# Pair stage of a four-layer graph network: part of the one-hot and row work moved from VectorE to ScalarE and GpSimd

## The reference

```python
def _sage(x, src, dst, Wn, bn, Wr):
    msg = x[src]
    agg = segment_sum(msg, dst, N)
    deg = segment_sum(ones, dst, N)
    mean = agg / maximum(deg, 1.0)[:, None]
    return mean @ Wn + bn + x @ Wr

h = relu(_sage(x, src, dst, W1n, b1n, W1r) + (x @ Wl1 + bl1))
out = _sage(h, src, dst, W2n, b2n, W2r) + (h @ Wl2 + bl2)
x = layernorm(x + out)
```

## Time and profile before

| | us |
|---|---|
| median of 3 runs | 3620.97 (3620.26 to 3625.03) |
| the profiled execution | 3621.94 |
| its span | 3620.1 |

### The profile page before, as it was taken

How to read it: one execution, slowest core, us unless ns; L and a number is a source line. 1 busy time by engine, 2 the same in 40 slices (tenths; PEclk the granted TensorE clock), 3 DMA queues, 4 the chain that set the end, 5 groups by cost and what they waited for, 6 DMA issues and landing times.

```text
span 3620.1 us, 122165 instructions
## 1 busy us (share of the span) xinstructions
PE 2921.0 (81%) x50473; PEld 2635.8 (73%) x50473; DVE 2935.5 (81%) x4757; ACT 2188.2 (60%) x5856; POOL 1429.5 (39%) x1204
## 2 busy tenths in 40 slices
PE   0199999999999789899787787887767888887886
PEld 0177777777777689899677777777756777777775
DVE  7599999999999733233588878988857999999997
ACT  6334444444444410000598888898867989899887
POOL 2000000000000000000298988998973666666564
PEclk9999999999999999999899999999977988889897
DMA  8157777777777799888687777887738888888884
GB/s 220 66 154 234 232 231 226 226 228 229 236 231 226 250 346 366 334 325 325 220 279 255 264 257 250 262 268 244 264 125 286 291 277 278 280 281 275 272 278 135
DMA packets 606666, 907.43 MB, mean 251 GB/s; under 512 B 358505, under 2 KB 494858, under 8 KB 587163
## 3 DMA queue, kind: packets, MB, share of 16 engines
q1 hardware_dynamic: 583992, 800.62, 67.7%
q10 hardware_dynamic: 19763, 94.38, 7.2%
q0 software_dynamic: 2352, 4.52, 0.3%
HBM read 651.96 MB, written 247.40 MB: 248 GB/s over the span
## 4 chain that ended last, share of the span: by engine, by line
DVE 37%; PE 28%; issue 12%; ACT 10%; DMA 7%; POOL 6%; ACTq 0%; DVEq 0%; SPq 0%; POOLq 0%
PE ps L1054 8%; PE ps L671 5%; DVE EDG L861 4%; DMA U<-AD 4%; DVE U L842 4%; DVE U L1824 3%; POOL EDG L1275 3%; ACT U L1634 3%; DVE EDG L1762 2%; PE ps L684 2%; PE ps L697 2%; ACT U L1336 2%; POOL EDG L1267 2%; DVE U L834 2%; PE ps L1296 2%
## 5 line engine op out<-in xcount | busy, mean ns | idle before, releaser
L561 ACT ACTIVATE U<-ps 128x512 bf16<-128x512 f32 (+1 forms) x637 | 356.3, 573 | 559.8 <-PE ps L684 535.6
L1634 ACT ACTIVATE U<-U,T 128x65 f32<-128x65 f32 x1806 | 460.1, 342 | 48.6 <-PE ps L1695 43.6
L1054 PE MATMUL ps<-U 128*128 128x192 bf16 x4802 | 418.0, 248 | 32.8 <-DMA U<-AD 32.4
L1267 POOL TENSOR_TENSOR EDG<-U,edge 128x512 f32<-128x512 f32 (+1 forms) x196 | 212.6, 1090 | 584.7 <-DVE edge L1419 550.8
L1054 PEld LDWEIGHTS ps<-U 128*128 128x128 bf16 x4802 | 402.8, 98 | 41.6 <-DMA U<-AD 38.4
L671 PE MATMUL ps<-U 128*128 128x98 bf16 (+1 forms) x5292 | 365.4, 224 | 34.1 <-DVE U L842 34.1
L671 PEld LDWEIGHTS ps<-U 128*128 128x128 bf16 x5292 | 339.4, 98 | 57.5 <-DVE U L842 55.6
L1662 POOL TENSOR_TENSOR U<-U 128x455 f32<-128x455 f32 x258 | 296.9, 1154 | 213.0 <-DVE U L1824 213.0
L861 DVE TENSOR_TENSOR EDG<-edge,EDG 128x1792 bf16<-128x1792 bf16 x343 | 366.2, 1079 | 13.7 <-DMA OSD<-EDG 12.4
L1303 PE MATMUL ps<-U 128*128 128x65 bf16 x7203 | 288.2, 195 | 73.8 <-DVE A L1396 72.8
L697 PE MATMUL ps<-EDG,U 128*128 128x193 bf16 x2401 | 311.5, 249 | 35.8 <-ACT U L561 24.6
(11 more groups left out here) (322 smaller groups left out, 6923.6 us busy)
## 6 DMA issues: line engine op xcount, KB each, us to landing
U<-ROWS SPq DMA_DIRECT2D x411, 448.0 KB, 4.7
U<-AD SPq DMA_DIRECT2D x98, 1568.0 KB, 8.5
OND<-EDG SPq DMA_DIRECT2D x343, 224.0 KB, 2.8
OSD<-EDG SPq DMA_DIRECT2D x343, 224.0 KB, 3.5
AD<-U ACTq DMA_DIRECT2D x49, 1568.0 KB, 5.5
EDG<-ROWS SPq DMA_DIRECT2D x171, 448.0 KB, 6.1
U<-OND SPq DMA_DIRECT2D x303, 224.0 KB, 5.7
U<-OSD SPq DMA_DIRECT2D x213, 224.0 KB, 4.8
```

What stands on the lines that cost most here:

```text
L561: ev4.by(act.activation(prow[i % NPW][:, P * g:P * (g + m)], ps[4 + gg % 2][:, 0:P * m], ACT.Copy))
L1054: ins = pe.matmul(ps[q][:, 0:192], arow[r][:, P * j:P * j + P], (XsB if p else XsA)[:, j, :, :].rearrange("p s f -> p (s f)"), start=(j == ...
L1634: ins = act.activation(V4[k % NV][:, 0, c, :], H[k % NHR][:, c, :], ACT.Copy, scale=a4[d % 2][:, s:s + 1])
```

## The change

Five pieces of work change their engine. The slot conversion of L850 goes to ScalarE, just ahead of L584 and L585. The mean of L878 goes to ScalarE, just behind the copy of X. Of the 14 one-hot columns of each `hots`, the last two of the target part, c = 5 and 6, are made by ScalarE as Relu(1 - |slot - r|): two Abs of 128 elements with the slot as pointer bias, a wait for its own engine, and one Relu over both. VectorE makes the other 12. Stores and counts wait for both. ScalarE copies the second half of the layer's output from PSUM to one of two new buffers (`xadd`), and GpSimd adds it to X, ahead of the bias. On VectorE the semaphore `summed` now comes with the reciprocal.

```diff
 pairs_sp:
+                sp.wait_ge(hot_b.at, hot_b.o + k + 1)
 pairs_pool, biased(i):
+                pool.wait_ge(t_out.at, i + 1)
+                x_in.by(pool.tensor_tensor(X[:, i, :], X[:, i, :], xadd[i % 2], ALU.add))
                 pool.wait_ge(x_in.at, i + 1)
 pairs_act, dense(i, n):
                     cat_x.by(act.activation(cat[q][:, D:P], X[:, i, :], ACT.Copy))
+                    act.wait_ge(summed.at, i + 1)
+                    cat_d.by(act.activation(cat[q][:, 0:D], A[:, i, 0:D], ACT.Copy, scale=rdeg[:, i:i + 1]))
...
-                    t_out.by(act.activation(T[:, i, 0:D], ps[7][:, 2 * P:2 * P + D], ACT.Copy))
+                    act.activation(T[:, i, 0:D], ps[7][:, 2 * P:2 * P + D], ACT.Copy)
+                    if i >= 2:
+                        act.wait_ge(x_in.at, i - 1)
+                    t_out.by(act.activation(xadd[q], ps[7][:, 2 * P + D:3 * P], ACT.Copy))
 pairs_act:
+            def hots(i, b):
+                k = NH7 * i + b
+                r = k % NHB
+                if k >= NHB:
+                    kk = k - NHB
+                    act.wait_ge(count4.at, NG4 * (kk // NH7) + (7 * (kk % NH7) + 6) // 4 + 1)
+                    act.wait_ge(hot_st[r].at, 32 * (k // NHB))
+                act.wait_ge(slot_ea.at, i + 1)
+                for c in (5, 6):
+                    ac.by(act.activation(OD[r][:, c, :], iota1, ACT.Abs, scale=-1.0, bias=E3[:, i, 1, 7 * b + c:7 * b + c + 1]))
+                act.wait_ge(ac.at, ac.n)
+                hot_b.by(act.activation(OD[r][:, 5:7, :], OD[r][:, 5:7, :], ACT.Relu, bias=1.0, scale=-1.0))
...
-                    act.wait_ge(slot_ev.at, e + 1)
+                    act.wait_ge(slot_mm.at, 2 * e + 2)
+                    if e >= 2:
+                        act.wait_ge(hot8.at, NH7 * (e - 1))
+                    slot_ev.by(act.activation(sdb[e % 2].rearrange("p b s c -> p s b c"),
+                                              bc(ps[3][:, 0:2 * NB].unsqueeze(2), [P, 2 * NB, 2]), ACT.Identity, bias=sc[:, 41:42]))
...
                     count(i, 2)
+                    hots(i, 2)
                 if d is not None:
                     dense(d, 3)
                     dense(d, 12)
                 if i is not None:
+                    hots(i, 3)
                     count(i, 3)
 pairs_pe, count(i, n):
                 pe.wait_ge(hot8.at, NH7 * i + (g + m - 1) // 7 + 1)
+                pe.wait_ge(hot_b.at, hot_b.o + NH7 * i + (g + m + 1) // 7)
 pairs_pe, dense, n == 2:
-                        pe.wait_ge(x_in.at, i)
+                        pe.wait_ge(t_out.at, i)
 pairs_dve:
-            def slots(e):
...
-                hot8.by(dve.tensor_tensor(HOT[r].rearrange("p s c (r k) -> p (s c) r k", k=2), bc(r1v.unsqueeze(1), [P, 14, D, 2]),
+                hot8.by(dve.tensor_tensor(HOT[r].rearrange("p s c (r k) -> p (s c) r k", k=2)[:, 0:12, :, :], bc(r1v.unsqueeze(1), [P, 12, D, 2]),
...
-                    summed.by(dve.tensor_scalar(nod[:, 1, i:i + 1], ps[6][:, 3 * D:XW], 1.0, None, ALU.max))
-                    dve.wait_ge(summed.at, i + 1)
-                    dv.by(dve.reciprocal(rdeg[:, i:i + 1], nod[:, 1, i:i + 1]))
-                elif n == 3:
...
-                    cat_d.by(dve.tensor_scalar(cat[q][:, 0:D], A[:, i, 0:D], rdeg[:, i:i + 1], None, ALU.mult))
-                elif n == 11:
-                    dve.wait_ge(t_out.at, i + 1)
-                    x_in.by(dve.tensor_tensor(X[:, i, :], X[:, i, :], ps[7][:, 2 * P + D:3 * P], ALU.add))
+                    summed.by(dve.reciprocal(rdeg[:, i:i + 1], nod[:, 1, i:i + 1]))
```

More of the change, by code:

```diff
@@ L469, in gnn_kernel @@
         x_ok = on(spl_a, 2)
+        hot_b = on(ld_x, 32)
+        xadd = [part(o2 + 6272 + D * i, D) for i in range(2)]
         over_in, over_t, bounds_t = sem("over_in"), sem("over_t"), sem("bounds_t")
@@ L575, in pairs_act @@
                     off_ev.by(act.activation(offb, ps[2][0:CP, 256:256 + NB], ACT.Identity, bias=sc[0:CP, 40:41]))
+                if i is not None:
+                    hots(i, 0)
                 if d is not None:
@@ L578, in pairs_act @@
                     count(d, 11)
+                if i is not None:
+                    hots(i, 1)
+                if d is not None:
                     count(d, 12)
@@ L601, in pairs_act @@
                     count(i, 4)
+                    hots(i, 4)
                 if d is not None:
@@ L605, in pairs_act @@
                     count(i, 5)
+                    hots(i, 5)
                 if d is not None:
@@ L609, in pairs_act @@
                     count(i, 6)
+                    hots(i, 6)
                     count(i, 7)
@@ L844, in fields @@
                 (fld_hot if c1 == HC else dv).by(ins)
-            def slots(e):
-                dve.wait_ge(slot_mm.at, 2 * e + 2)
-                if e >= 2:
-                    dve.wait_ge(hot8.at, NH7 * (e - 1))
-                slot_ev.by(dve.tensor_scalar(sdb[e % 2].rearrange("p b s c -> p s b c"),
-                                             bc(ps[3][:, 0:2 * NB].unsqueeze(2), [P, 2 * NB, 2]), -1.0, None, ALU.add))
             def hots(i, b):
@@ L860, in hots @@
                     dve.wait_ge(hot_st[r].at, 32 * (k // NHB))
-                hot8.by(dve.tensor_tensor(HOT[r].rearrange("p s c (r k) -> p (s c) r k", k=2), bc(r1v.unsqueeze(1), [P, 14, D, 2]),
-                                          bc(sdb[i % 2][:, b, :, :].rearrange("p s (c k) -> p (s c) k", k=2).unsqueeze(2), [P, 14, D, 2]),
+                hot8.by(dve.tensor_tensor(HOT[r].rearrange("p s c (r k) -> p (s c) r k", k=2)[:, 0:12, :, :], bc(r1v.unsqueeze(1), [P, 12, D, 2]),
+                                          bc(sdb[i % 2][:, b, :, :].rearrange("p s (c k) -> p (s c) k", k=2)[:, 0:12, :].unsqueeze(2), [P, 12, D, 2]),
                                           ALU.is_equal))
@@ L870, in dense @@
                     dv.by(dve.tensor_copy(deg[:, i:i + 1], ps[6][:, 3 * D:XW]))
[L871 to L876 removed]
+                    dv.by(dve.tensor_scalar(nod[:, 1, i:i + 1], ps[6][:, 3 * D:XW], 1.0, None, ALU.max))
                     own()
[L878 to L881 removed]
+                    summed.by(dve.reciprocal(rdeg[:, i:i + 1], nod[:, 1, i:i + 1]))
             for t in range(LAST):
@@ L899, in pairs_dve @@
                             fields(jb, (3, 8).index(n), 5, HC)
-                    if e is not None and n == 1:
-                        slots(e)
-                    if d is not None and n < 11:
+                    if d is not None:
                         dense(d, n)
@@ L905, in pairs_dve @@
                         hots(i, (n + 1) // 2)
-                    if d is not None and n == 11:
-                        dense(d, n)
             dve.wait_ge(x_ok.at, x_ok.o + NB)
```

2 lines of the change are left out of this document (removed).

## The result

The changed kernel took 3644.33 us (median of 4 runs, 3643.74 to 3651.91), the kernel before 3622.41 beside it (4 runs, 3620.26 to 3625.03). The ratio is 1.0064, interval 1.0048 to 1.008: slower by 22 us. The forecast was 3657 (+36), range 3585 to 3682.

A forecast was written before the change was run, and what follows sets the result against it. VectorE was taken as full, TensorE close behind and waiting on ScalarE's evictions. 20.46 + 0.88 + 0.32 + 0.93 = 22.59 us a step against 21.80, +0.79 over 45 steps, gave 3657 us; range 3585 to 3682, the forecast's own 3638 to 3680.

The forecast's parts named there:

- Limits: Pair-stage step of 21.80 us: VectorE's own limit falls to 20.3 us, TensorE's without waits for VectorE is 20.46.
- TensorE's removable wait: TensorE's loads waiting for VectorE's field products (L842) and source one-hots (L820): 1.34 us a step would go.
- Term 1: Run offsets: first hot pair between offset copy and count group 10 eviction delays TensorE's use by 0.88 us a step.
- Term 2: Slot numbers: ScalarE's slot conversion lengthens the gapless chain to the load TensorE waits for by 0.32 us a step.
- Term 3: Row transfers: ROWS issues hold ScalarE, delaying the fourth pair and count group 3 eviction; +0.93 us a step.
- c: Start of ScalarE's count 1 eviction, the zero point for the times in the row-transfer chain.
- it lasts 1.20: Length in us taken for the second ROWS issue, read from the kernel before the change; it would end at c + 3.22.
- The other four pairs: Remaining hot pairs on ScalarE, behind the count 3 eviction: priced zero, or 0.2 us a step if cover is thinner.
- No change: Rival A: ROWS issues do not hold up the fourth pair; 3619 us, within 3605 to 3630; chance 0.17.
- Faster: Rival B: ScalarE's extra work does not reach TensorE; 3561 us in full, 3591 by half; chance 0.23.

The follow-up runs named there:

- the early pair: Changed kernel with ScalarE's first pair of one-hot columns moved to the step's start, before the eviction of count group 9; 3612.71 us, ratio 0.9969.
- idle-place run: Changed kernel with the two ROWS stores issued behind the eviction of count group 7, where ScalarE idles; 3634.53 us, ratio 1.0032.
- without the split: Changed kernel, but VectorE makes all 14 one-hot columns; slots, means and output add stay where the change puts them; 3586.54 us, ratio 0.9898.
- AD store on SyncE, late slots: Changed kernel with first pair at the step's start, slot conversion behind count group 7, and SyncE issuing the AD store; 3613.2 us, ratio 0.9975.
- late slots: Changed kernel with first pair at the step's start and slot conversion made from SBUF behind count group 7; 3615.21 us, ratio 0.9985.
- split only: Changed kernel with one-hots still split, but slot numbers, means and output add back on VectorE; 3648.86 us, ratio 1.0071.
- AD store on SyncE: Changed kernel with the 1568 KB AD store issued by SyncE instead of ScalarE; 3651.89 us, ratio 1.0088.
- the run above: Kernel before the change with GpSimd's bias add one step later, behind the next block's gather; 3615.26 us, ratio 0.9996.

## Why the prediction was right in its sign and too large in its size

*Limits.* VectorE is busy 271.6 us of 300 at a step of 22.33, that is 20.2 us a step (forecast 20.3). TensorE's removable wait was taken as 1.34 us a step, from the waits for L842 and L820. The field products' part, 1.18, went. The 0.16 at the offset matmuls stayed (`PEld ps L674 <- issue`, 6.5 us in 40 times) although it read L820 before: it was not VectorE's. This step of the forecast was 0.16 too kind.

*Term 1*, +0.88 forecast, +0.88 measured (1.17 less 0.29), and the early pair took exactly this wait away. The pair costs 581.24 - 580.21 = 1.03, as computed, and the Abs starts 0.21 after the offset copy, forecast 0.19. In the one odd step of 40 the Abs starts 0.37 after the copy; why stays open.

*Term 2*, +0.32 forecast, +0.30 measured. Right.

*Term 3*, +0.93 forecast, +0.30 measured: here the mechanism was right and the size wrong. The chain up to the first ROWS issue came out within 0.02 (c = 609.27, issue forecast at c + 1.72 = 610.99, measured 610.97). The hold is real: the next Abs starts 0.12 behind the issue's end, and with the issue elsewhere the step is 0.33 shorter. The Trainium skill (Advanced Engine Details and Errata, Sequencer Loop) says other engine instructions can be queued while a control instruction executes; queued or not, none started here before 611.86. The failed step was "it lasts 1.20": a length measured at one distance from another transfer, carried to another distance. It took 0.59, and the 0.61 less is nearly all of the error in the term (0.63). Before, it stood 2.13 us behind the AD store, now 4.31. In the mean of all steps the wait is 0.35.

*The other four pairs* were priced at zero, with 0.2 us a step "if that cover is thinner". The wait of a pair for the store out of its ring buffer was in no term. It shows 17 times, 10.9 us in 900, and with the longer ROWS issues it makes the mean step 0.17 longer than the usual one.

*Sum with the measured sizes*: 0.88 + 0.30 + 0.30 - 1.18 = +0.30 a step, or 22.11 us, against 22.16 in the undisturbed steps. With the 0.17 of the disturbed ones it is +0.47, against +0.52 in the mean. The remaining 0.05 is not assigned.

That the forecast came as near as it did is partly luck: term 3 was 0.63 too large, and 0.16, 0.17 and 0.05 were missing elsewhere. With term 3 alone put right the sum gives 0.79 - 0.63 = +0.16 a step, 7 us, and the change would have been called hardly slower.

*Rivals.* No change (the issue doesn't hold) is refuted by the idle-place run. Faster (ScalarE's load is absorbed) was to decide at terms under 1.34: they came to 1.48. The kernel with the early pair shows the other side of that condition: without term 1 what is left is well under 1.34, and it is 0.3% faster. So the sign hung on where one pair stood. What I did not weigh at all was that 0.70 us a step was to be had without the split.

## What to carry to other kernels

Here the full engine could be relieved of its small instructions (slots, mean, add: 0.70 us of a 21.8 us step with the 0.12 at the source one-hots, 1.0% of the kernel) while its large ones stayed; work moved to an engine that is half idle cost its full length where the bottleneck waited for that engine's next result. Before moving work, list the moments at which the receiving engine is waited for, and price each moment by itself, including the transfers that it issues there. Take the length of a DMA issue only from rows at the same distance from the large transfers around it, and count a reading over all steps before you build on one of them.

## What the runs showed of the hardware that was not expected

**A DMA issue can be long while large stores are in flight.** The second ROWS issue (24.5 KB), by its start after the issue of the 1568 KB AD store, one step of each profile, and the median of all steps from 300 to 1200 us with the shortest and longest:

| kernel | AD store on | starts after it, us | lasts | ends after it | all steps |
|---|---|---|---|---|---|
| before | ScalarE | 2.13 | 1.20 | 3.33 | 1.20 (0.91 to 1.56) |
| AD store on SyncE, late slots | SyncE | 3.74 | 1.21 | 4.95 | 1.19 (1.15 to 1.34) |
| late slots | ScalarE | 4.00 | 1.03 | 5.03 | 1.00 (0.90 to 1.25) |
| split only | ScalarE | 4.00 | 0.90 | 4.90 | 0.92 (0.82 to 1.26) |
| AD store on SyncE | SyncE | 4.11 | 0.92 | 5.03 | 0.79 (0.74 to 1.19) |
| changed | ScalarE | 4.31 | 0.59 | 4.90 | 0.58 (0.44 to 1.05) |
| early first pair | ScalarE | 4.32 | 0.82 | 5.14 | 0.73 (0.60 to 1.14) |
| ROWS in idle place | ScalarE | 12.4 | 0.33 | 12.7 | 0.33 (0.32 to 0.54) |

In these steps it lasts 1.2 us at most, and otherwise until 4.9 to 5.1 us after the store's issue (the distance isn't all: two kernels with the same 4.3 us have 0.59 and 0.82); the store lands 5.5 to 6.8 us after its issue in the median. Starting the issue 0.3 us earlier gained nothing there, and so 0.3 us saved ahead of it were lost twice (split only, late slots). The issue is long whichever engine issued the store. That agrees with the Trainium skill (DMA: Bandwidth & Descriptors, Issuing engines are not separate DMA queues), which says that DMAs started by ScalarE, SyncE or GpSimd all run on the same 16 DMA engines. That the store causes it is inferred from the moments; a kernel without the store was not run. The last block of the idle-place run shows that the store alone is not enough:

```profile
1267.37 0.48 SPq L488 DMA_DIRECT2D OSD<-EDG  x1
...
1271.93 0.35 ACTq L587 DMA_DIRECT2D AD<-U  x1
...
1276.16 0.35 ACTq L561 DMA_DIRECT2D ROWS<-EDG  x1
```

The AD store issued at 1271.93 lands 5.8 us later, so it is still in flight, yet 4.23 us behind it the ROWS issue takes 0.35 us, where the changed kernel has 0.59 at 4.31. What differs there is that SyncE issues no one-hot store any more. The load of all stores together fits this better than the AD store by itself; no run separates them, and why the issue rarely lasts over 1.2 us stays open too.

**GpSimd and VectorE wait for each other.** In the kernel before, GpSimd's bias add meets the source one-hot:

```profile
614.28 0.31 POOL L492 TENSOR_TENSOR X<-X,brow 128x64 f32<-128x64 f32 x1 [13.47 <-DVE X L881]
614.33 1.20 DVE L820 TENSOR_TENSOR U<-iota,EDG 128x1764 bf16<-128x1764 bf16 x1
```

With the add one step later that one-hot takes 1.08 us (median of the run above). The other way round, in the kernel without the split:

```profile
615.51 1.08 DVE L867 TENSOR_TENSOR EDG<-edge,EDG 128x1792 bf16<-128x1792 bf16 x1
615.91 2.56 POOL L493 TENSOR_TENSOR X<-X,U 128x64 f32<-128x64 f32 x1 [5.96 <-ACT U L550]
616.51 1.78 DVE L855 TENSOR_TENSOR U<-U 128x3136 bf16<-128x3136 bf16 x1
618.21 1.13 DVE L838 TENSOR_REDUCE EDG<-ps 128x10 bf16<-128x490 f32 x2
618.55 0.32 POOL L495 TENSOR_TENSOR X<-X,brow 128x64 f32<-128x64 f32 x1
```

GpSimd's first add lasts 2.56 us (median of the 49: 2.55), until VectorE has gone from products in SBUF to a reduction that reads PSUM; the second add, of the same size, takes 0.32 beside that reduction. The Trainium skill (SBUF — State Buffer, SBUF: two separate sides) calls the shared port pair an exclusive lock and "not a bandwidth split", and says that the one that comes second fully blocks. The trace agrees for GpSimd. For VectorE it shows less: the one-hot that started 0.05 us after an add of 0.31 lost only 0.12 us. The forecast costed the output add on GpSimd at nothing, which held, since nobody waits for it for several us.
